# Keys of a gated delta rule turned by VectorE and a DMA through HBM instead of TensorE

## The chip, the cores and the metric

One core of a Trainium2 chip runs the whole kernel. The metric is the device time of one execution in microseconds (us), the median of several runs: 1523.45 us before the change (three runs, 1520.14 to 1526.65).

## What is computed

The input is x of 8 batches x 512 rows x 128 columns, all in f32. The output is

```
x = x + 0.5 * ffn(layernorm(x))        # gated: silu(x w1) * (x w2), two gelu layers of 512, back to 128
x = x + attn_block(layernorm(x))
x = x + 0.5 * ffn(layernorm(x))

attn_block(x):                         # 8 heads of 128
  n = layernorm(x)
  q, k = l2norm(silu(n Wq)), l2norm(silu(n Wk));  v = silu(n Wv)
  beta, alpha = sigmoid(n Wb), sigmoid(n Wa)
  per head and row t:  S = alpha (S - beta k (k S)) + beta k v;   o_t = S q_t
  x = x + o Wo
  x = x + gelu(layernorm(x) W1 + b1) W2 + b2
```

## The kernel before

**Chunks.** The recurrence is not run row by row. The 512 rows of a batch are cut into NC = 4 chunks of 128 rows (c = 0 to 3). For each chunk and each of the 8 heads the kernel forms the 128x128 products of keys with keys and of keys with queries, decays them, inverts the triangular matrix of the keys (on blocks of 32x32 on GpSimd, joined by TensorE), and then needs only a few 128x128 products per chunk to carry the state. A group g (0 or 1) is half of the heads, four, and fills one bank of PSUM.

**Stages.** Batches are worked in a software pipeline written out by hand, one queue of instructions for each engine. `SP(s, p, f1)` is the central stage: it runs the attention of batch s (solve, state, output: "S") and at the same time prepares batch p = s + 1 (projections, norms, keys: "P"); then come `F1(f1)` and `F2(s)`, the two feed-forward parts with the MLP, the products of keys with queries and the joins of the inverse among them. There are six such stages with p = 1 to 6 and f1 = p + 1, and one with p = 7 and no f1. Stage p = 1 follows a differently ordered first batch. SP has a first part (c = 0) and three steps (c = 1, 2, 3).

**TensorE in a step** (`SP_step`), each entry for both groups: products of keys with the state (L1386), projections of k (L1344), key products `keys_keys(p, c-1)` (L1364), `solve` (L1395), products of the state with the queries (L1412), `update` (L1403, not in c = 3), projections of q, `output` (L1422), projections of v, in c = 3 the turn of the next batch's input (L1231), `turn(p, c)` (L1356, 8 transposes of the keys against the identity), `attend` (L1431, the output projection). `SP_last` goes on with `keys_keys(p, 3)`, the four pairs of layer-1 products of f1 (L1267), the turn of the layer norm's rows xa (L1231), then the slots of F1. `layer1(…, 1)` waits for `attended` of c = 3 (its bank), `layer1(…, 2)` for the first gating.

**VectorE in a step**: `rhs` (L877), `squares` (L731 and three small ones: sums of squares of the keys of c and the queries of c - 1), `decayed_k(p, c-1)` (L843, key products times decays into R, R is also what `solve` reads), `new_state` (L885 and L889), `unit_k(p, c)` (L745: keys times 1/norm), `unit_q(p, c-1)` (L752, and then L757, a turn of 32x32 blocks of 128x1024 into the buffer mid), `attended` (L899). After step 3: moments of the layer norm (L590 to L603, L574 to L584), gating 0 (L641), rows xa (L609), gating 1, `decayed_k(p, 3)`, gating 2 and 3.

**GpSimd in a step**: `norm` (L482, a power), `scaled_k` (L501: keys times decays into KD, not in c = 3), `mask` (L491: growth rows plus the mask into MT; waits for the rows' DMA and for `output` of the same chunk). **ScalarE**: silu of k, `solved` (L1104), silu of q, output copies (L1109), silu of v, `copy_T` (L1098, turned keys from PSUM to KT), `decays` (L1082, eight exps on MT, waits for the mask).

**SP**, the queue of all DMAs, in order: for each c the blocks of R to HBM (L338), `q_store` (L355: mid to q_rows), growth rows (L330), `q_load` (L362: four loads that place the 32x32 blocks in QET so that the full turn is complete). The queries have gone this way already; the keys are turned on TensorE.

## Time and profile before

| what | value |
|---|---|
| profiled execution | 1525.31 us, of it 1523.6 us from the first to the last instruction |
| median of three runs | 1523.45 us |
| TensorE busy | 1447.8 us (95%); VectorE 810.8 (53%), ScalarE 692.2 (45%), GpSimd 566.2 (37%) |
| chain that ended last | TensorE 52%, issue 15%, GpSimd 13%, VectorE 12%, ScalarE 6% |
| granted TensorE clock | 0.974 of 2.4 GHz in the mean |
| stages p = 2 to 6 | the second half of layer 1 (L1267) starts at 441.20, 617.93, 794.67, 971.40 and 1148.12 us |
| DMA | 96.73 MB, 25.2% of the 16 engines' span |

Busy time is the union of an engine's instructions; that of TensorE includes time in which matmuls only drain. An f32 product of 128x128 is two matmul instructions in the trace, a transpose is one. An entry such as "[0.59 <-DVE big L641]" is the idle time of the engine ahead of the instruction and the instruction that ended it.

### The profile page before, as it was taken

To read this page: it belongs to the slowest core of one execution; us is meant where nothing else is said; L and a number is where in the kernel's file an instruction comes from. 1 tells how busy PE (TensorE), PEld (TensorE's weight loads), DVE (VectorE), ACT (ScalarE), POOL (GpSimd) and SP (SyncE) were. 2 spreads that over 40 slices of the span, in tenths; PEclk is the share of its full clock that TensorE was granted. 3 is DMA by queue.
4 is the path that set the end of the run, shared out by engine and by line. 5 is a ranking of instruction groups with operands and counts; after the bars stand their busy time and mean duration, and the time that the engine had idled before them with its cause. 6 is when DMAs were issued, how large, how long until landed. Compare 5 with 4: busy or idle time off the path is not lost.

```text
span 1523.6 us, 26080 instructions
## 1 busy us (share of the span) xinstructions
PE 1447.8 (95%) x10334; PEld 993.3 (65%) x10334; DVE 810.8 (53%) x2405; ACT 692.2 (45%) x1182; POOL 566.2 (37%) x641
## 2 busy tenths in 40 slices
PE   7997889999999999999999999999999999879968
PEld 3455776557866588566875578665885668645934
DVE  3566357553674556743674536654666436741330
ACT  2566256225662356424662266523664256622222
POOL 0037033741438124550338314471346504482000
PEclk9999699999999999999999999999999999889979
DMA  5122013230233214430232313331133302413000
GB/s 169 64 75 48 21 53 83 73 80 22 78 90 77 46 39 92 101 80 23 60 79 70 81 36 81 83 79 33 39 91 94 80 23 61 93 49 74 8 0 7
DMA packets 243338, 96.73 MB, mean 63 GB/s; under 512 B 212528, under 2 KB 227600, under 8 KB 243216
## 3 DMA queue, kind: packets, MB, share of 16 engines
q1 hardware_dynamic: 243216, 95.06, 25.2%
q8 instruction: 82, 1.34, 0.4%
q14 instruction: 40, 0.33, 0.1%
HBM read 65.43 MB, written 29.61 MB: 62 GB/s over the span
## 4 chain that ended last, share of the span: by engine, by line
PE 52%; issue 15%; POOL 13%; DVE 12%; ACT 6%; DMA 2%; SPq 0%; POOLq 0%; DVEq 0%; ACTq 0%
PE bank L1238 18%; PE bank L1344 4%; PE bank L1267 4%; POOL blkT L528 3%; POOL blkP L525 3%; PE bank L1246 3%; PE bank L1395 2%; DVE bst L731 2%; ACT MT L1082 2%; PE bank L1422 2%; POOL MT L491 2%; PE bank L1378 2%; PE bank L1431 2%; PE bank L1403 2%; PE bank L1614 1%
## 5 line engine op out<-in xcount | busy, mean ns | idle before, releaser
L1238 PE MATMUL bank<-big,h 128*128 128x512 f32 x992 | 447.0, 596 | 0.0
L1238 PEld LDWEIGHTS bank<-big,h 128*128 128x128 f32 x992 | 181.6, 190 | 197.0 <-issue 195.6
L482 POOL TENSOR_TENSOR rnorm<-ssq,mhalf 128x16 f32<-128x16 f32 (+1 forms) x35 | 84.0, 2401 | 539.4 <-DVE ssq L740 539.4
L1344 PE MATMUL bank<-wqkv,nT 128*128 128x512 f32 x336 | 161.5, 600 | 0.0
L528 POOL TENSOR_TENSOR blkT<-blkT,blkP 128x31 f32<-128x31 f32 (+15 forms) x248 | 135.9, 548 | 19.4
L525 POOL TENSOR_TENSOR blkP<-blkA,blkT 128x31 f32<-128x31 f32 (+15 forms) x248 | 126.4, 510 | 34.8 <-DMA blkA<-blocks_out 15.8
L1267 PE MATMUL bank<-xT,w 128*128 128x512 f32 x256 | 121.7, 622 | 7.6 <-ACT xT L996 4.2
L870 DVE TENSOR_SCALAR TB<-bank 32x512 f32<-32x512 f32 (+1 forms) x48 | 33.1, 689 | 144.6 <-PE bank L1656 64.8
L1013 ACT ACTIVATE big<-bank,cols 128x512 f32<-128x512 f32 x64 | 43.0, 686 | 138.3 <-PE bank L1238 100.4
L1020 ACT ACTIVATE big<-bank,cols 128x512 f32<-128x512 f32 x64 | 43.1, 686 | 108.6 <-PE bank L1238 108.5
L849 DVE TENSOR_TENSOR MT<-bank,MT 128x512 f32<-128x512 f32 x56 | 38.6, 691 | 99.6 <-PE bank L1378 99.6
L1267 PEld LDWEIGHTS bank<-xT,w 128*128 128x128 f32 x256 | 48.4, 200 | 65.2 <-issue 49.9
L1082 ACT ACTIVATE MT<-MT,biasj 128x128 f32<-128x128 f32 x256 | 78.3, 389 | 9.9 <-POOL MT L491 9.5
L509 POOL TENSOR_TENSOR QET<-QET,sgf 128x1024 f32<-128x1024 f32 x21 | 49.3, 2349 | 89.7 <-DMA sgf<-e_rows 89.7
L1344 PEld LDWEIGHTS bank<-wqkv,nT 128*128 128x128 f32 x336 | 57.0, 192 | 37.4 <-issue 36.8
L731 DVE BATCH_NORM_STATS2 bst<-big 128x6 f32<-128x128 f32 x224 | 46.0, 279 | 53.4 <-ACT big L1092 53.4
L1092 ACT ACTIVATE QET<-bank 128x512 f32<-128x512 f32 x56 | 33.5, 597 | 87.8 <-PE bank L1344 87.8
L491 POOL TENSOR_TENSOR MT<-rows_or_g,maskf 128x1024 f32<-128x1024 f32 x28 | 69.7, 2488 | 3.0 <-PE bank L1422 3.0
L1246 PE MATMUL bank<-w,big 128*128 128x128 f32 x512 | 68.2, 279 | 2.3 <-DVE TB L870 1.5
L1246 PEld LDWEIGHTS bank<-w,big 128*128 128x128 f32 x512 | 62.6, 192 | 11.8 <-issue 8.4
L1422 PEld LDWEIGHTS bank<-MT,V 128*128 128x128 f32 x512 | 61.8, 192 | 12.9 <-issue 12.9
L1395 PE MATMUL bank<-V,R 128*128 128x128 f32 x512 | 64.9, 281 | 2.8 <-DVE TB L870 1.6
(212 smaller groups left out, 2704.2 us busy)
## 6 DMA issues: line engine op xcount, KB each, us to landing
rows_or_g<-g_rows SPq DMA_DIRECT2D x28, 512.0 KB, 4.0
q_rows<-mid SPq DMA_DIRECT2D x28, 512.0 KB, 2.7
QET<-q_rows SPq DMA_DIRECT2D x112, 128.0 KB, 4.1
sgf<-e_rows SPq DMA_DIRECT2D x21, 512.0 KB, 4.7
blocks_out<-R SPq DMA_DIRECT2D x128, 32.0 KB, 1.7
blkA<-blocks_out SPq DMA_DIRECT2D x8, 512.0 KB, 3.2
t_back<-blkT SPq DMA_DIRECT2D x8, 512.0 KB, 2.6
r_back<-blkA SPq DMA_DIRECT2D x8, 512.0 KB, 3.0
```

The lines of the kernel that those rows point to most:

```text
L482: pool.tensor_tensor(rnorm[:, heads_of], ssq[:, heads_of], mhalf[:, :].to_broadcast([128, heads_of.stop - heads_of.start]), ALU.pow).then_ ...
L491: pool.tensor_tensor(MT[:, u, :], grow, maskf[:, :].unsqueeze(1).to_broadcast([128, H, 128]), ALU.add).then_inc(d_mask, 1)
L525: pool.tensor_tensor(prod, A3[:, j, j + 1:].unsqueeze(2).to_broadcast([128, n, m]), T3[:, j:j + 1, 0:m].to_broadcast([128, n, m]), ALU.mul ...
L528: pool.tensor_tensor(T3[:, j + 1:, 0:m], T3[:, j + 1:, 0:m], prod, ALU.subtract).then_inc(b_prod, 1)
L731: last = dve.bn_stats(bst[:, i, :], krow[g][:, i, :] if i < H else QET[:, H * (g - 1) + i - H, :])
L1082: last = act.activation(MT[:, u, :], MT[:, u, :], ACT.Exp, bias=biasj[:, u:u + 1])
L1238: last = pe.matmul(bank[bk + i][:, :], w[:, k, 128 * o:128 * o + 128], src[:, k, :], start=(k == 0), stop=(k == KB - 1))
L1246: last = pe.matmul(bank[4][:, 128 * c:128 * c + 128], src[:, k, 128 * c:128 * c + 128], w[:, k, :], start=(k == 0 and c == 0), stop=(k == ...
L1267: pe.matmul(bank[bk][:, :], w[:, 128 * o:128 * o + 128], xT[:, :], start=True, stop=True).then_inc(f["gate"], 1)
L1344: pe.matmul(bank[4 + n % 2][:, :], nT[:, 128 * c:128 * c + 128], wqkv[:, i // 2, 512 * (i % 2):512 * (i % 2) + 512], start=True, stop=True ...
L1395: last = pe.matmul(heads(bank[g])[:, h, :], R[:, u, :], V[:, u, :], start=True, stop=True)
L1422: last = pe.matmul(heads(bank[2 + g])[:, h, :], V[:, u, :], MT[:, u, :], start=(c == 0 and h == 0), stop=True, skip_group_check=True)
```

## The change

For the batches p = 1 to 7, all chunks but the last of the last batch (`at_end`), the keys no longer pass through TensorE and ScalarE. After `unit_k`, VectorE turns the 32x32 blocks of the keys into the chunk's part of R, which `solve` of batch s has read by then; SP stores it to a new tensor k_rows in HBM (`k_store`) and loads it back into KT by blocks (`k_load`, four DMAs). `keys_keys` waits for these loads. It is moved behind `update` in the steps c = 1 and 2, behind the projections of q in step 3, and, for chunk 3, from the head of `SP_last` to between the third and the fourth pair of layer-1 products. On VectorE `decayed_k` is moved behind `new_state`. The semaphores a_sq and a_sk become one counter each instead of four.

```diff
+def at_end(b, c):
+    return (b, c) == (B - 1, NC - 1)
...
+            def k_store(b, c):                                          # SP
+                sp.wait_ge(k_turned, (b - 1) * NC + c + 1)
+                sp.dma_start(k_rows[c, :, :], R[:, H * c:H * c + H, :].rearrange("p h n -> p (h n)")).then_inc(k_out, 16)
+            def k_load(b, c):
+                sp.wait_ge(k_out, 16 * ((b - 1) * NC + c + 1))
+                if c > 0:
+                    sp.wait_ge(s_ks, (b - 1) * 6 + 2 * c)
+                blocked = k_rows[c, :, :].rearrange("(r x) (u k p) -> k x u r p", r=NBLK, u=H, k=NBLK)
+                for k in range(NBLK):
+                    sp.dma_start(KT[BS * k:BS * k + BS, H * c:H * c + H, :].rearrange("x u (r p) -> x u r p", r=NBLK),
+                                 blocked[k]).then_inc(k_in[c % 2], 16)
...
             def P(b):
-                grow_in(b, 1)
+                k_store(b, 0), k_load(b, 0), grow_in(b, 1)
                 for c in range(1, NC):
                     blocks(b, c - 1)
+                    if not at_end(b, c):
+                        k_store(b, c)
                     q_store(b, c - 1)
+                    if not at_end(b, c):
+                        k_load(b, c)
...
             def unit_k(b, c):                                           # VectorE
...
+                if at_end(b, c):
+                    return
+                dve.wait_ge(p_unit, b * NC + c + 1)
+                dve.wait_ge(s_w, (b - 1) * 8 + 2 * c + 2)
+                dve.transpose(R[:, H * c:H * c + H, :].rearrange("p h n -> p (h n)"), krow[c].rearrange("p h n -> p (h n)")
+                              ).then_inc(k_turned, 1)
...
             def SP_step(s, p, c):                                       # VectorE
                 rhs(s, c, 0), rhs(s, c, 1)
                 if p is not None:
-                    squares(p, c), decayed_k(p, c - 1)
+                    squares(p, c)
                 if c < NC - 1:
                     new_state(s, c, 0), new_state(s, c, 1)
                 if p is not None:
+                    decayed_k(p, c - 1)
                     unit_k(p, c), unit_q(p, c - 1)
                 attended(s, c)
...
-                    copy_T(p, c, 0), copy_T(p, c, 1), decays(p, c)      # ScalarE, SP_step; SP_first alike
+                    if at_end(p, c):
+                        copy_T(p, c, 0), copy_T(p, c, 1)
+                    decays(p, c)
...
             def keys_keys(b, c, g):                                     # TensorE
-                pe.wait_ge(p_trc, 2 * NC * (b + 1) + 2 * c + g + 1)
+                if at_end(b, c):
+                    pe.wait_ge(p_trc, 4 * NC + g + 1)
+                elif g == 0:
+                    pe.wait_ge(k_in[c % 2], 16 * NBLK * (2 * (b - 1) + c // 2 + 1))
+                if c > 0:
+                    pe.wait_ge(p_dk, b * 2 * NC + 2 * c - 1 + g)
+                else:
+                    pe.wait_ge((j_dve, j_act)[g], b * NS)
...
             def SP_step(s, p, c, f1):
                 state_keys(s, c, 0), state_keys(s, c, 1)
                 if p is not None:
-                    proj(p, c, 2), proj(p, c, 3), keys_keys(p, c - 1, 0), keys_keys(p, c - 1, 1)
+                    proj(p, c, 2), proj(p, c, 3)
...
                 if c < NC - 1:
                     update(s, c, 0), update(s, c, 1)
+                elif p is not None:
+                    proj(p, c, 0), proj(p, c, 1)
                 if p is not None:
+                    keys_keys(p, c - 1, 0), keys_keys(p, c - 1, 1)
+                if c < NC - 1 and p is not None:
                     proj(p, c, 0), proj(p, c, 1)
                 output(s, c, 0), output(s, c, 1)
...
-                    turn(p, c, 0), turn(p, c, 1)
+                    if at_end(p, c):
+                        turn(p, c, 0), turn(p, c, 1)
                 attend(s, c)
...
             def SP_last(s, p, f1):
-                if p is not None:
+                if f1 is None and p is not None:
                     keys_keys(p, NC - 1, 0), keys_keys(p, NC - 1, 1)
                 if f1 is not None:
                     layer1("f1", f1, 0)
                     pe.wait_ge(s_xa, s * NC + NC)
-                    layer1("f1", f1, 1), layer1("f1", f1, 2), layer1("f1", f1, 3)
+                    layer1("f1", f1, 1), layer1("f1", f1, 2), keys_keys(p, NC - 1, 0), keys_keys(p, NC - 1, 1)
+                    layer1("f1", f1, 3)
```

## Rows read from the trace of the kernel before

**Rows 1.** The page, part 1: busy us (share of the span) and instructions.
```profile
PE 1447.8 (95%) x10334; PEld 993.3 (65%) x10334; DVE 810.8 (53%) x2405; ACT 692.2 (45%) x1182; POOL 566.2 (37%) x641
```

**Rows 2.** TensorE's groups by line: count, busy us, mean ns, idle before.
```profile
L1356 PE MATMUL bank<-ident,big 128*128 128x128 f32 x224 | 30.0, 278 | 7.1 <-DVE R L870 3.8 <-DVE big L745 3.4
```

**Rows 3.** Timeline of TensorE, stage p = 3: start us, us, line.
```profile
574.45 1.95 PE L1431 MATMUL bank<-wo,blkA 128*128 128x128 f32 x16
...
592.98 1.95 PE L1431 MATMUL bank<-wo,blkA 128*128 128x128 f32 x16
...
609.29 1.04 PE L1356 MATMUL bank<-ident,big 128*128 128x128 f32 x8
610.16 1.95 PE L1431 MATMUL bank<-wo,blkA 128*128 128x128 f32 x16
611.95 1.95 PE L1364 MATMUL bank<-KT 128*128 128x128 f32 x16
613.74 3.60 PE L1267 MATMUL bank<-xT,w 128*128 128x512 f32 x8
617.93 3.70 PE L1267 MATMUL bank<-xT,w 128*128 128x512 f32 x8 [0.59 <-DVE big L641]
621.47 0.60 PE L1231 MATMUL bank<-ident,xa 128*128 128x128 f32 x4
```

**Rows 4.** The chain of waits, 545 to 640 us, in order of time.
```profile
581.71 3.20 DVE bst L731 x16
...
588.76 1.23 DVE big L745
...
592.83 2.36 POOL MT L491
...
600.10 3.20 DVE bst L731 x16
...
604.04 2.92 POOL rnorm L482
...
608.12 3.39 DVE QET L752
611.54 1.25 DVE mid L757
...
617.12 0.76 DVE big L641
```

**Rows 5.** Timelines of VectorE and GpSimd, end of stage p = 1.
```profile
252.55 3.36 DVE L745 TENSOR_TENSOR big<-big,rnorm 128x1024 f32<-128x1024 f32 x1 [1.82 <-POOL rnorm L482]
...
252.48 2.34 POOL L491 TENSOR_TENSOR MT<-rows_or_g,maskf 128x1024 f32<-128x1024 f32 x1
```

**Rows 6.** Timelines of VectorE and GpSimd, 626 to 629 us.
```profile
626.36 2.29 DVE L752 TENSOR_TENSOR QET<-QET,rnorm 128x1024 f32<-128x1024 f32 x1 [1.76 <-POOL rnorm L482]
...
627.52 1.22 POOL L525 TENSOR_TENSOR blkP<-blkA,blkT 128x31 f32<-128x31 f32 x1
```

**Rows 7.** Timelines of TensorE and GpSimd, stage p = 1.
```profile
195.03 1.94 PE L1356 MATMUL bank<-ident,big 128*128 128x128 f32 x8 [3.77 <-DVE R L870]
...
255.96 1.09 PE L1356 MATMUL bank<-ident,big 128*128 128x128 f32 x8 [2.81 <-DVE big L745]
...
199.71 1.90 POOL L501 TENSOR_TENSOR KD<-big,kds 128x1024 f32<-128x1024 f32 x1 [10.42 <-issue]
```

**Rows 8.** Windows of 2 us: busy us of each engine, then granted clock, DMA.
```profile
192.00:194.00 2.00, 0.00 (x0) 0.00 (x0) 1.96 (x5) 0.00 (x0) 0.00 (x0) 0.84 0.00 0
...
198.00:200.00 2.00, 2.00 (x12) 2.00 (x11) 0.00 (x0) 1.57 (x5) 0.29 (x1) 0.50 0.01 4
...
254.00:256.00 2.00, 0.04 (x1) 0.04 (x1) 2.00 (x2) 0.00 (x0) 0.82 (x1) 1.00 0.00 0
```

**Rows 9.** DMA: SP's timeline, and the page's issues with us to landing.
```profile
615.84 2.80 SPq L362 DMA_DIRECT2D QET<-q_rows  x4
...
QET<-q_rows SPq DMA_DIRECT2D x112, 128.0 KB, 4.1
```

More of the change, by code:

```diff
@@ L193, in build_program @@
         g_rows = nc.dram_tensor("g_rows", [U, C], f32).ap()
+        k_rows = nc.dram_tensor("k_rows", [NC, 128, H * 128], f32).ap()
         q_rows = nc.dram_tensor("q_rows", [NC, 128, H * 128], f32).ap()
@@ L238, in build_program @@
         a_unit, a_qnorm, a_knorm = sem("a_unit"), sem("a_qnorm"), sem("a_knorm")
-        a_sq, a_sk = ([sem(f"a_{k}{i}") for i in range(4)] for k in ("sq", "sk"))
+        a_sq, a_sk = sem("a_sq"), sem("a_sk")
         a_gate, a_rows = ([sem(f"a_{k}{c}") for c in range(NC)] for k in ("gate", "rows"))
@@ L247, in build_program @@
         q_in = [sem("q_in0"), sem("q_in1")]
+        k_turned, k_out = sem("k_turned"), sem("k_out")
+        k_in = [sem("k_in0"), sem("k_in1")]
         n_eT, e_out, e_in, s_sq = sem("n_eT"), sem("e_out"), sem("e_in"), sem("s_sq")
@@ L765, in moments0 @@
                 if c == NC - 1:
-                    last.then_inc((a_sq, a_sk)[x][0], 1)
+                    last.then_inc((a_sq, a_sk)[x], 1)
             def norms0(x):
                 done = (a_sq, a_sk)[x]
-                dve.wait_ge(done[0], 1)
-                dve.tensor_tensor(bsq0, bst0[:, :, 1::3], bst0[:, :, 1::3], ALU.mult).then_inc(done[1], 1)
-                dve.wait_ge(done[1], 1)
+                dve.wait_ge(done, 1)
+                dve.tensor_tensor(bsq0, bst0[:, :, 1::3], bst0[:, :, 1::3], ALU.mult).then_inc(done, 1)
+                dve.wait_ge(done, 2)
                 dve.scalar_tensor_tensor(out=bsq0, in0=bsq0, scalar=64.0, in1=bst0[:, :, 2::3],
-                                         op0=ALU.mult, op1=ALU.add).then_inc(done[2], 1)
-                dve.wait_ge(done[2], 1)
+                                         op0=ALU.mult, op1=ALU.add).then_inc(done, 1)
+                dve.wait_ge(done, 3)
                 ssq_x, rnorm_x = (z[:, x, :, :].rearrange("p c h -> p (c h)") for z in (ssq0, rnorm0))
                 dve.scalar_tensor_tensor(out=ssq_x, in0=bsq0[:, :, 0], scalar=EPS_L2, in1=bsq0[:, :, 1],
-                                         op0=ALU.add, op1=ALU.add).then_inc(done[3], 1)
-                dve.wait_ge(done[3], 1)
+                                         op0=ALU.add, op1=ALU.add).then_inc(done, 1)
+                dve.wait_ge(done, 4)
                 rsqrt((a_qnorm, a_knorm)[x], 0, ssq_x, rnorm_x, rs_ta[:, :], rs_tb[:, :])
@@ L1096, in copy_T @@
                 u = slice(H * c + 4 * g, H * c + 4 * g + 4)
-                act.wait_ge(p_tr, 2 * NC * (b + 1) + 2 * c + g + 1)
+                act.wait_ge(p_tr, 4 * NC + g + 1)
                 act.activation(KT[:, u, :], heads(bank[6 + g]), ACT.Copy).then_inc(p_trc, 1)
@@ L1178, in SP_first @@
                 if p is not None:
-                    silu(p, 0, 4), silu(p, 0, 5), copy_T(p, 0, 0), copy_T(p, 0, 1)
+                    silu(p, 0, 4), silu(p, 0, 5)
                     if p == 1:
@@ L1350, in turn, with keys_keys @@
                     pe.wait_ge(p_unit, b * NC + c + 1)
+                pe.wait_ge(p_dk, b * 2 * NC + 2 * c - 1 + g)
+                for h in range(4):
+                    last = pe.transpose(bank[6 + g][:, 128 * h:128 * h + 128], krow[c][:, 4 * g + h, :], ident[:, :])
+                last.then_inc(p_tr, 1)
+            def keys_keys(b, c, g):
+                if at_end(b, c):
+                    pe.wait_ge(p_trc, 4 * NC + g + 1)
+                elif g == 0:
+                    pe.wait_ge(k_in[c % 2], 16 * NBLK * (2 * (b - 1) + c // 2 + 1))
                 if c > 0:
@@ L1354, in turn @@
                     pe.wait_ge((j_dve, j_act)[g], b * NS)
-                for h in range(4):
-                    last = pe.transpose(bank[6 + g][:, 128 * h:128 * h + 128], krow[c][:, 4 * g + h, :], ident[:, :])
-                last.then_inc(p_tr, 1)
-            def keys_keys(b, c, g):
-                pe.wait_ge(p_trc, 2 * NC * (b + 1) + 2 * c + g + 1)
                 for h in range(4):
@@ L1456, in SP_first @@
                 if p is not None:
-                    proj(p, 0, 4), proj(p, 0, 5), turn(p, 0, 0), turn(p, 0, 1)
+                    proj(p, 0, 4), proj(p, 0, 5)
                 attend(s, 0)
```

## The prediction
> **What bounds the kernel now.** I read the page first: TensorE is busy for 95% of the span [rows 1], and the turns of the keys are one of its groups [rows 2]. That suggests that whatever TensorE is spared comes off the time. The view that decides is the chain of waits over one of the repeating stages (prepare batch p beside attention of batch s = p - 1). I take p = 3, from 545 to 640 us; stages p = 2 to 6 repeat every 176.7 us to within 0.1 us.
>
> In the steps c = 1 and 2 TensorE is full: from one output projection (L1431) to the next it takes 592.98 - 574.45 = 18.53 us [rows 3]. But the chain does not run through it. It is a loop over three engines: squares of the keys on VectorE (L731), norms on GpSimd (L482), `unit_k` (L745), scaled keys on GpSimd (L501), mask (L491), exps and the next silus on ScalarE, squares again. From squares to squares it takes 600.10 - 581.71 = 18.39 us [rows 4], only 0.14 less than TensorE's step, with hardly a wait in it. After the last step (c = 3) the chain stays on VectorE: norms end at 606.96, then `unit_k`, `unit_q` (held until the mask is done, 3.39 us instead of 1.22), the block turn of the queries (1.25), `attended`, the moments of the layer norm and the first gating, which starts at 617.12 [rows 4]. Only then can TensorE run the second pair of layer-1 products: it idled 0.6 us before them, from 617.34 to 617.93 [rows 3]. So the end of a stage is set by VectorE's chain, and TensorE is covered up to there by work that it has to do anyway.
>
> **The change part by part.**
>
> *Turns removed from TensorE.* 27 of 28 chunks lose 8 transposes: 610.16 - 609.29 = 0.87 us each time [rows 3], 23.5 us in all, and the waits ahead of them, 7.1 us in sum, all of it in stage p = 1 [rows 2]. In stages 2 to 6 that is 4 x 0.87 = 3.5 us before TensorE reaches the first layer-1 products; it comes there too early, because the first gating doesn't move forward. ScalarE's copies of KT go too; they lie in the time in which it waits for the mask, and I cost them at nothing.
>
> *Block turn added to VectorE.* `unit_k` is followed by a 128x1024 block turn, and `unit_q`, the queries' own turn and `attended` stand behind it in the queue. The same operation took 1.25 us in each case [rows 4]. It works beside GpSimd undisturbed, so scaled keys can start as before. In steps 1 and 2 VectorE has room: `attended` comes some 2 us later, at about TensorE's next products with the state, and `rhs` still ends before `solve` needs it by a few tenths. In step 3 there is no room. Norms end at 607.0 as before (I add 0.1 for the drift of two rounds). `output` is now done before that, so GpSimd's mask no longer waits for it, but takes the memory first, and `unit_k` is held. That is the order of stage p = 1, where the mask began at 252.48 and `unit_k`, begun at 252.55, took 3.36 us [rows 5]. So: norms 607.1, mask and `unit_k` +3.4 = 610.5, block turn +1.2 = 611.7, `unit_q` +1.2 = 612.9, its turn +1.2 = 614.1, against 612.7 before. Mask, `unit_k` and `unit_q` cost the same in either order; the difference is the added turn: +1.4 us with the drift.
>
> *The wait moved in front of layer 1.* From there the moments and the gating take as long as before: gating starts at 614.1 + 4.4 = 618.5, and its product pair on TensorE at 619.3 instead of 617.93. Before it, TensorE is done with the output projection between 608.5 (all 3.5 us saved) and 609.4 (a wait of 0.8 us before `update` in step 2, where ScalarE's silus end late for the earlier TensorE). It does one layer-1 pair (1.72), waits for `attended` until 614.4, does the second pair, waits again for the gating until 619.3: two gaps of about 3.3 and 3.2 us, where there was one of 0.6.
>
> *Key products moved.* The products of chunk 3 took 613.74 - 611.95 = 1.79 us ahead of layer 1 [rows 3]; there they filled the time in which the gating was made. Now they stand between the third and the fourth layer-1 pair, behind the gating. The stretch behind it grows from 3.45 to 3.45 + 1.79 us. So TensorE leaves the stage at 619.3 + 5.24 = 624.55 instead of 621.4: +3.15 us. In steps 1 to 3 the products move by a few places within one full queue; they are worth nothing there. Behind the stage TensorE is full and the inversion and its transfers have room, so 3.15 us stay.
>
> *Transfers.* A chunk adds a store of 512 KB and four loads of 128 KB on SP's queue. k_load stands behind q_store, which waits for the queries' turn. In steps 1 and 2 the loads can go out some 0.5 us after that turn; they take 2.8 us to issue [rows 9] and 4.1 us to land [rows 9], about 1 to 2 us before the moved products want them. For chunk 3 the loads start at 614.6, the last at 616.7, and land at 620.8; they are wanted at 621.0. I take nothing; the bounds are 0 and 2 us per stage. The growth rows, now behind k_load, have 8 us of room.
>
> *Stages p = 1 and 7.* In p = 1 the scaled keys started at 199.71, because an exp stood behind the copies of KT, and these behind the turn at 195.03 [rows 7]. Without it they can start when `unit_k` ends, at 194.3: the loop starts 5.4 us earlier. At the stage's end 0.2 of it goes to VectorE's longer chain and 1.8 to the moved products: -3.4 us (bounds: 0 and -7.1, all the waits before turns). In p = 7 the last turn stays on TensorE and waits for a held `unit_k`: +0.7 us (bounds 0 and 3).
>
> *Clock.* With an idle time of 3.77 us before the turn at 195.03 the granted clock fell from 2.4 to 1.2 GHz within the wait (0.84 in one window, 0.50 in the next ones) and stayed there until about 200.1: 5.1 us of work at half rate, 2.5 us lost [rows 7, 8]. With 2.81 us before the turn at 255.96 it did not fall [rows 7, 8]. The new gaps of 3.3 and 3.2 us with 1.7 us of work between them lie between these two. The cost is 0 to 2.5 us per stage for six stages; I take the middle, 1.25 each, 7.5 us. The Trainium skill (TensorE: Matmul & The Clock Gate, Part 1) says "the default state is throttled, and activity releases the throttle", and advises against idle gaps between bursts of matmuls; by that rule all six stages pay in full, +15 us in place of 7.5.
>
> *Sum*, against the profiled execution's own 1525.31 us (span 1523.6): -3.4 + 5 x 3.15 + 0.7 = +13.0, clock +7.5, together +20.5: 1545.8. The median of the runs is 1.9 us below that execution, so the forecast is 1544 us.
>
> **The rivals.**
>
> *A, faster: TensorE is the bound and what it is spared counts.* Then 23.5 + 7.1 = 30.6 us go: 1493 us. For it: 95% busy and a chain with 52% on TensorE. Against it: the chain of the stage's end is VectorE's, and the products that follow the gating have become more. It decides if the first gating comes at least 1.8 us earlier than now; nothing on its chain gets shorter. 10%.
>
> *B, no change: the memory goes to GpSimd twice in a row.* In steps 1 and 2 `unit_q` now waits while the scaled keys run, and the mask is queued right behind them. At 626.36 in the same situation VectorE got its turn in between: GpSimd's next operation of 31 elements, begun at 627.52, took 1.22 us [rows 6]. If the mask went first instead, the loop would win about 0.9 us a round, norms of step 3 would end some 1.7 us earlier, and a stage would cost 1.4 us instead of 3.15: -3.4 + 7 + 0.7 = +4.3, 1528 us without a fallen clock. 10%.
>
> *C, slower still: the keys come late.* SP issues in order and the two stores and eight loads of a step meet in the DMA engines. If the loads of chunk 3 land 2 us late in six stages, the time is 1544 + 12 = 1556 us. For it: a margin of 0.2 us there. Against it: loads of the same pattern from q_rows took 4.1 us in the median over 112 [rows 9]. 18%. The Trainium skill (VectorE: DVE Perf Modes, The three transpose paths) warns that a plain DMA copy that turns by its access pattern is 19 times slower than the crossbar's turn. By it every product of keys would wait for tens of us and the kernel would be far slower than here; the loads from q_rows, whose shortest runs are the same, show no such thing, and I give it less than 1% inside C.
>
> **How the numbers follow.** Forecast 62%, with its own range of 1536.5 (the clock never falls) to 1551.5 (it falls in all six); A 10%, B 10%, C 18%. A measurement of this kernel tells about 0.5% (7.6 us) from no change. A is the case faster; B lies within it; the forecast and C are slower: 0.10, 0.10, 0.80. The range from 1526 to 1560 leaves out A and the upper end of C.
>
> **What would show it.** Right: per stage two idle times of TensorE on the L1267 products, one released by VectorE's `attended` (L899) or its successor, one by the gating (L641), together 5 to 7 us where 0.6 stood; `unit_k` of step 3 held to about 3.4 us; the period of stages 2 to 6 grown from 176.7 to between 179.9 and 182.4 us; squares to squares still 18.4 us; a granted clock below 1.0 in slices that now show 9s. Wrong: L641 releasing TensorE no later than now relative to the stage's start; a period under 176.7; waits of the key products on the loads of KT in steps 1 and 2 above 1 us; or `rhs` late enough to hold `solve` by more than 1 us, which would raise the price of the added turn beyond mine.

## The result, and the profile after

The changed kernel is slower: 1549.45 us (median of 4 runs, 1548.85 to 1554.82) beside 1524.22 us for the kernel before (median of 4), ratio 1.0176 with a 95% interval of 1.0144 to 1.0208. The forecast was 1544 us, with a range of 1526 to 1560. From the first to the last instruction, the profiled execution of after takes 1547.1 us; before took 1523.6, so 23.5 us are to be explained.

The page of after, part 1, answers to [rows 1]. The 27 turns are gone from TensorE (216 instructions, 23.5 us), but its busy time fell by only 5.3 us:

```profile
PE 1442.5 (93%) x10118; PEld 976.4 (63%) x10118; DVE 850.7 (55%) x2432; ACT 662.1 (43%) x1128; POOL 565.8 (37%) x641
```

TensorE's groups by line (count, busy us, mean ns, then the idle time before them by releaser). L1303 are the layer-1 products (L1267 of before), L1404 the key products (L1364):

```profile
L1303 PE MATMUL bank<-xT,w 128*128 128x512 f32 x256 | 137.8, 681 | 34.8 <-DVE xa L932 18.7 <-DVE big L668 11.9 <-ACT xT L1030 4.2
...
L1404 PE MATMUL bank<-KT 128*128 128x128 f32 x448 | 58.0, 285 | 0.3 <-DMA KT<-k_rows 0.3
```

The 7.1 us of idle time ahead of the turns [rows 2] are gone, and ahead of layer 1 TensorE waits 30.6 us for VectorE, 18.7 released by `attended` (L932) and 11.9 by the gating (L668). Before had 7.6 us of idle time there in all, 4.2 of it the same wait for ScalarE. For the keys through HBM, TensorE waited 0.3 us in the whole program.

TensorE's timeline at the end of stage p = 3 (start us, us; in brackets the idle time ahead and its releaser), which answers to [rows 3]:

```profile
610.16 0.60 PE L1267 MATMUL bank<-ident,xin 128*128 128x128 f32 x4
610.60 1.95 PE L1471 MATMUL bank<-wo,blkA 128*128 128x128 f32 x16
612.39 1.88 PE L1303 MATMUL bank<-xT,w 128*128 128x512 f32 x4
617.41 1.98 PE L1303 MATMUL bank<-xT,w 128*128 128x512 f32 x4 [3.14 <-DVE xa L932]
622.32 3.18 PE L1303 MATMUL bank<-xT,w 128*128 128x512 f32 x4 [2.93 <-DVE big L668]
625.29 2.48 PE L1404 MATMUL bank<-KT 128*128 128x128 f32 x16
627.61 1.88 PE L1303 MATMUL bank<-xT,w 128*128 128x512 f32 x4
629.33 0.60 PE L1267 MATMUL bank<-ident,xa 128*128 128x128 f32 x4
```

Two gaps of about 3 us, the products between them, and a third pair that takes 3.18 us where the second took 1.98. VectorE over the same time, answering to the end of [rows 4]:

```profile
610.14 3.38 DVE L772 TENSOR_TENSOR big<-big,rnorm 128x1024 f32<-128x1024 f32 x1 [1.82 <-POOL rnorm L509]
613.55 1.25 DVE L778 STREAM_TRANSPOSE R<-big 128x1024 f32<-128x1024 f32 x1
614.72 1.18 DVE L785 TENSOR_TENSOR QET<-QET,rnorm 128x1024 f32<-128x1024 f32 x1
615.94 1.25 DVE L790 STREAM_TRANSPOSE mid<-QET 128x1024 f32<-128x1024 f32 x1
617.11 0.25 DVE L932 TENSOR_TENSOR xa<-bank,xa 128x128 f32<-128x128 f32 x1
...
621.52 0.75 DVE L668 SCALAR_TENSOR_TENSOR big<-bank,cols,sgf 128x512 f32<-128x512 f32 x1
```

and GpSimd, in step 1 and at the end of the stage:

```profile
574.68 1.90 POOL L528 TENSOR_TENSOR KD<-big,kds 128x1024 f32<-128x1024 f32 x1 [1.49 <-DVE big L772]
576.54 3.35 POOL L518 TENSOR_TENSOR MT<-rows_or_g,maskf 128x1024 f32<-128x1024 f32 x1
...
607.20 2.91 POOL L509 TENSOR_TENSOR rnorm<-ssq,mhalf 128x16 f32<-128x16 f32 x1 [8.86 <-DVE ssq L767]
610.07 2.36 POOL L518 TENSOR_TENSOR MT<-rows_or_g,maskf 128x1024 f32<-128x1024 f32 x1
```

The mask starts 0.07 us ahead of `unit_k`, which takes 3.38 us instead of 1.22; the turn, `unit_q` and the second turn follow one behind the other. In windows of 2 us the granted clock (the first number behind the engines' busy times) falls right behind the second gap, from 2.4 to 1.2 GHz, that is from 1.0 to 0.5:

```profile
621.00:623.00 2.00, 0.68 (x2) 0.44 (x3) 1.90 (x8) 0.00 (x0) 0.00 (x0) 0.99 0.96 150
623.00:625.00 2.00, 2.00 (x4) 0.75 (x3) 0.95 (x3) 0.69 (x1) 0.00 (x0) 0.50 1.13 153
625.00:627.00 2.00, 2.00 (x12) 1.71 (x11) 0.02 (x1) 0.00 (x0) 0.00 (x0) 0.65 0.95 112
```

It is like this in stages p = 3 and 4. In the four others the clock fell in or right behind the first gap, of 2.6 us (p = 1) or 3.2 us (p = 2, 5, 6), before the second had begun. In p = 2, 5 and 6 it was still low for the third pair. TensorE in p = 2, where the granted clock is 0.50 from 436 to 444 us:

```profile
434.58 3.17 PE L1303 MATMUL bank<-xT,w 128*128 128x512 f32 x4 [3.25 <-DVE xa L932]
439.50 3.78 PE L1303 MATMUL bank<-xT,w 128*128 128x512 f32 x4 [1.75 <-DVE big L668]
```

A landmark makes the kernels comparable: the turns of `xin` on TensorE (610.16 here) split a stage into its full part and its end, which closes with the turns of `xa` (629.33). The table has stage p = 3 of every kernel and the mean of the four periods from p = 2 to p = 6, both from the one profiled execution, and the medians of all executions:

| kernel | xa to xin | xin to xa | mean period | median us (before beside it) | ratio, 95% interval |
|---|---|---|---|---|---|
| before | 164.11 | 12.62 | 176.73 | | |
| after | 162.43 | 19.17 | 182.00 | 1549.45 (1524.22) | 1.0176, 1.0144 to 1.0208 |
| e1 | 161.49 | 15.20 | 177.53 | 1521.31 (1523.25) | 0.998, 0.9967 to 0.9994 |
| e2 | 164.11 | 12.83 | 176.95 | 1528.39 (1523.25) | 1.0033, 1.002 to 1.0045 |
| e3 | 164.11 | 14.42 | 179.37 | 1539.57 (1523.25) | 1.0117, 1.0085 to 1.0148 |
| e4 | 162.34 | 17.86 | 180.17 | 1537.93 (1523.25) | 1.0102, 1.0076 to 1.0128 |
| e5 | 162.32 | 18.33 | 180.30 | 1536.37 (1522.62) | 1.0094, 1.0064 to 1.0124 |
| e6 | 162.32 | 16.33 | 179.91 | 1538.30 (1522.62) | 1.0097, 1.0078 to 1.0116 |
| e7 | 162.96 | 15.20 | 178.11 | 1529.72 (1522.62) | 1.0039, 1.0021 to 1.0058 |
| e8 | 163.67 | 12.91 | 176.40 | 1517.14 (1522.62) | 0.9951, 0.9933 to 0.9969 |
| e9 | 164.27 | 12.48 | 177.68 | 1530.24 (1523.89) | 1.0042, 1.0026 to 1.0058 |
| e10 | 163.43 | 12.91 | 176.10 | 1516.55 (1523.89) | 0.9945, 0.9928 to 0.9963 |
| e11 | 162.98 | 13.04 | 175.99 | 1513.50 (1523.89) | 0.9923, 0.9908 to 0.9938 |
| e12 | 164.11 | 12.48 | 176.60 | 1520.06 (1522.83) | 0.998, 0.9966 to 0.9994 |

After is 1.68 us shorter in the full part and 6.55 us longer at the end. The experiments ask what makes the end.

One caution for reading two traces against each other. The first batch, up to the first projections of stage p = 1 (L1344 at 189.27 us in before, L1380 at 188.79 in after), does the same work in all kernels. Yet in the profiled executions it ends anywhere from 185.3 us (e4) to 194.0 (e3), and the granted clock fell in it at different times. So the differences of stages below are counted from that point on.

### The profile page after: what moved, and what is told of

Read it like the earlier page. It is cut to its first block, busy times and chain, and to the rows that moved or that the text cites. A ratio compares the mean times of both kernels' runs of the same rounds, so it can differ in the third digit from the quotient of the medians.

```text
span 1547.1 us, 25805 instructions
## 1 busy us (share of the span) xinstructions
PE 1442.5 (93%) x10118; PEld 976.4 (63%) x10118; DVE 850.7 (55%) x2432; ACT 662.1 (43%) x1128; POOL 565.8 (37%) x641
## 3 DMA queue, kind: packets, MB, share of 16 engines
q1 hardware_dynamic: 359424, 123.38, 34.3%
q8 instruction: 80, 1.31, 0.3%
## 4 chain that ended last, share of the span: by engine, by line
issue 37%; POOL 29%; PE 19%; DVE 10%; ACT 4%; DMA 2%; POOLq 0%; DVEq 0%; ACTq 0%
POOL blkT L555 7%; PE bank L1274 7%; POOL blkP L552 6%; POOL rnorm L509 5%; POOL MT L518 4%; POOL QET L536 3%; POOL KD L528 2%; DVE bst L758 2%; PE bank L1303 2%; DVE big L772 2%; ACT MT L1116 1%; DMA sgf<-e_rows 1%; PE bank L1282 1%; PE bank L1571 1%; POOL blkA L558 1%
## 5 line engine op out<-in xcount | busy, mean ns | idle before, releaser
L1303 PE MATMUL bank<-xT,w 128*128 128x512 f32 x256 | 137.8, 681 | 34.8 <-DVE xa L932 18.7
L1380 PE MATMUL bank<-wqkv,nT 128*128 128x512 f32 x336 | 161.5, 600 | 0.0
L1303 PEld LDWEIGHTS bank<-xT,w 128*128 128x128 f32 x256 | 50.8, 213 | 98.3 <-issue 50.7
L1380 PEld LDWEIGHTS bank<-wqkv,nT 128*128 128x128 f32 x336 | 57.0, 192 | 37.4 <-issue 35.4
L518 POOL TENSOR_TENSOR MT<-rows_or_g,maskf 128x1024 f32<-128x1024 f32 x28 | 79.8, 2850 | 0.0
L1435 PEld LDWEIGHTS bank<-V,R 128*128 128x128 f32 x512 | 63.2, 196 | 15.0 <-issue 12.5
L1282 PEld LDWEIGHTS bank<-w,big 128*128 128x128 f32 x512 | 62.6, 192 | 11.8 <-issue 8.4
```

The source lines that it names most:

```text
L518: pool.tensor_tensor(MT[:, u, :], grow, maskf[:, :].unsqueeze(1).to_broadcast([128, H, 128]), ALU.add).then_inc(d_mask, 1)
L1282: last = pe.matmul(bank[4][:, 128 * c:128 * c + 128], src[:, k, 128 * c:128 * c + 128], w[:, k, :], start=(k == 0 and c == 0), stop=(k == ...
L1303: pe.matmul(bank[bk][:, :], w[:, 128 * o:128 * o + 128], xT[:, :], start=True, stop=True).then_inc(f["gate"], 1)
L1380: pe.matmul(bank[4 + n % 2][:, :], nT[:, 128 * c:128 * c + 128], wqkv[:, i // 2, 512 * (i % 2):512 * (i % 2) + 512], start=True, stop=True ...
L1435: last = pe.matmul(heads(bank[g])[:, h, :], R[:, u, :], V[:, u, :], start=True, stop=True)
```

## The experiments

**e1: before without the turns.** TensorE's turns and ScalarE's copies are left out from batch 1 on, so the key products use old keys.

```diff
-                    turn(p, c, 0), turn(p, c, 1)
-                    ... copy_T(p, c, 0), copy_T(p, c, 1), decays(p, c)
+                    ... decays(p, c)
```

> The kernel before without any turn of the keys of batches 1 to 7 on TensorE and without ScalarE's copies of them (left out: KT keeps the first batch's keys, so the products of the later batches use those). Nothing is put on VectorE or the DMAs. If the end of a stage is set by VectorE's chain, the 3.5 us that TensorE is spared in each of the stages 2 to 6 buy nothing there (second layer-1 pair still 176.7 us apart) and only stage 1 wins, about 5 us: 1518 us. If TensorE is the bound (rival A), 23.5 + 7.1 us go: 1493 us.

Measured 1521.31, ratio 0.998. Freeing TensorE of all turns is worth 2 us, not 30: the first theory is held, rival A falls. The 2 us are a difference of two effects. In the profiled executions stage p = 1 got 6.3 us shorter, and p = 2 to 6 got 4.9 us longer together, because the clock fell in p = 2, 4 and 6 (1.7 us each). TensorE in stage p = 3, where it held:

```profile
604.76 2.05 PE L1369 MATMUL bank<-KT 128*128 128x128 f32 x16 [1.78 <-DVE big L745]
...
612.25 3.70 PE L1267 MATMUL bank<-xT,w 128*128 128x512 f32 x8 [2.01 <-DVE big L641]
```

The full part became 2.62 us shorter (three turns of 0.87), the end 2.58 us longer: what TensorE is spared ahead of VectorE's chain it spends in waiting for that chain.

**e2: before with the block turn added.** TensorE still turns the keys; VectorE turns them as well, behind `unit_k`.

```diff
                 dve.tensor_tensor(krow[c], krow[c], rnorm... ).then_inc(p_unit, 1)
+                dve.wait_ge(p_unit, b * NC + c + 1)
+                dve.wait_ge(s_w, (b - 1) * 8 + 2 * c + 2)
+                dve.transpose(R[...], krow[c]...).then_inc(k_turned, 1)
```

> The kernel before, turns on TensorE kept, with the added block turn of 128x1024 behind unit_k on VectorE (written into R, read by nothing). VectorE's chain at a stage's end is 1.25 us longer, and the first gating and the stage end 1.3 us later in each of five stages, 0.5 to 1.3 in the other two: 1523.5 + 8 = 1531 us. If VectorE's added work is hidden, 1524 us.

Measured 1528.39. It lies between the two, but the trace decides against the theory's reason: a steady stage grew by 0.22 us, not by 1.25. Of the rest, 3.1 us lie in stage p = 1: an idle time of 5.03 us ahead of the first turn replaced the 3.77 of [rows 7], and the clock fell behind a wait of 2.98 us, where before it held behind 2.81. VectorE and GpSimd at the end of p = 3:

```profile
612.19 1.22 DVE L746 TENSOR_TENSOR big<-big,rnorm 128x1024 f32<-128x1024 f32 x1 [1.79 <-POOL rnorm L483]
613.45 1.25 DVE L750 STREAM_TRANSPOSE R<-big 128x1024 f32<-128x1024 f32 x1
614.62 2.11 DVE L757 TENSOR_TENSOR QET<-QET,rnorm 128x1024 f32<-128x1024 f32 x1
```

```profile
612.44 3.20 POOL L492 TENSOR_TENSOR MT<-rows_or_g,maskf 128x1024 f32<-128x1024 f32 x1 [0.29 <-PE bank L1428]
```

Here the mask still waits for `output` and comes behind `unit_k`. It runs while VectorE turns, and `unit_q`, which the mask would have held for 2.2 us in any case [rows 4], is held for only 0.9 us. From the end of the norms to the start of `attended` it is 5.78 us, against 5.77 in before and 7.00 in after.

**e3: before with the key products of chunk 3 moved** between the third and the fourth layer-1 pair.

```diff
-                    keys_keys(p, NC - 1, 0), keys_keys(p, NC - 1, 1)
                 if f1 is not None:
-                    ... layer1("f1", f1, 2), layer1("f1", f1, 3)
+                    ... layer1("f1", f1, 2), keys_keys(p, NC - 1, 0), keys_keys(p, NC - 1, 1)
+                    layer1("f1", f1, 3)
```

> The kernel before with one edit: the key products of chunk 3 stand between the third and fourth layer-1 pair instead of at the head of SP_last. TensorE waits for the first gating 0.6 + 1.8 = 2.4 us instead of 0.6, and the stage ends 1.8 us later, six times: 1523.5 + 10.7 = 1534 us. If the products only change places within a full queue, 1524 us.

Measured 1539.57, 5 to 6 us more than the theory's. TensorE:

```profile
630.73 1.98 PE L1267 MATMUL bank<-xT,w 128*128 128x512 f32 x4 [2.40 <-DVE big L641]
632.55 1.95 PE L1364 MATMUL bank<-KT 128*128 128x128 f32 x16
```

The products left a gap of 2.40 us where 0.59 stood and cost their 1.8 us behind it. The remainder is the clock, as far as the trace shows: in three of the five stages p = 2 to 6 the stretch from the third pair to the turns of `xa` took 7.0 us, in the other two 5.32. The trace is of the slowest of four executions (1547.85 us), and 4.8 us of its excess lie in the first batch.

**e4: after with both gaps filled** by three products of 128x512 each, whose results nobody reads.

```diff
                     layer1("f1", f1, 0)
+                    pe.wait_ge(p_dk, p * 2 * NC + 2 * NC - 2)
+                    filler(3)
                     pe.wait_ge(s_xa, s * NC + NC)
-                    layer1("f1", f1, 1), layer1("f1", f1, 2), keys_keys...
+                    layer1("f1", f1, 1), filler(3), layer1("f1", f1, 2), keys_keys...
```

> The changed kernel with three products of 128x512 of constant data (weights w1 and w2 into a bank that is free) in each of the two gaps of TensorE ahead of attended and of the first gating: 2.6 us of work in gaps of 3.2 and 2.9 us. If the gaps themselves cost nothing beyond VectorE's chain but let the clock fall, the clock stays at 2.4 GHz there and what half rate cost comes back: the five stages 2 to 6 repeat every 179.9 us instead of 181.6 to 182.9, about 10 to 13 us in all, 1538 us. If the clock costs nothing, 1549 us; if the filler delays TensorE, more.

Measured 1537.93, 11.5 us under after with more work. Between the profiled executions it is 13.5 us, 3.5 of them in the first batch, so some 10 us are what the clock cost. From 240 to 1330 us the granted clock is 1.00, and the pairs behind the gaps take 1.98 us in each stage:

```profile
610.75 1.98 PE L1303 MATMUL bank<-xT,w 128*128 128x512 f32 x4 [0.64 <-DVE xa L932]
...
615.66 1.98 PE L1303 MATMUL bank<-xT,w 128*128 128x512 f32 x4 [0.35 <-DVE big L668]
```

**e5: after, the mask of chunk 3 behind `unit_k`.**

```diff
                 pool.wait_ge(s_o, s * 8 + 2 * c + 2)
+                if c == NC - 1:
+                    pool.wait_ge(p_unit, b * NC + c + 1)
                 pool.tensor_tensor(MT[:, u, :], grow, maskf... )
```

> After, with one wait more: GpSimd's mask of chunk 3 also waits for unit_k(3), so that VectorE scales the keys first, turns them while GpSimd works, and only then scales the queries. In the trace of after GpSimd's mask (610.07) stood ahead of unit_k (610.14, 3.38 us), and turn, unit_q and turn followed one behind the other; in the run with a turn added to the kernel before, where unit_k came ahead of the mask, the added turn cost 0.2 us a stage. Theory: the turn costs its 1.25 us only because of that order. Then unit_k(3) takes 1.18, the turn lies under the mask, and the attended rows come about 1.2 us earlier in each of six stages: 1549.5 - 7 = 1542 us, with attended at about 1.0 us after the end of the queries' turn as now. Rival: the turn costs 1.25 us in whatever order (VectorE's own time is the bound), or the mask's later end holds ScalarE's exponentials and with them the silu of layer 1: no change, 1549, or slower, 1553.

Measured 1536.37: one wait more gives 13 us. VectorE, end of p = 3:

```profile
605.83 1.23 DVE L774 TENSOR_TENSOR big<-big,rnorm 128x1024 f32<-128x1024 f32 x1 [1.82 <-POOL rnorm L509]
607.09 1.25 DVE L780 STREAM_TRANSPOSE R<-big 128x1024 f32<-128x1024 f32 x1
608.26 2.41 DVE L787 TENSOR_TENSOR QET<-QET,rnorm 128x1024 f32<-128x1024 f32 x1
```

The turn lies under the mask (607.23, 2.36 us), as in e2; norms to `attended` went from 7.00 to 6.08 us and the first gap from 3.14 to 2.31. The mechanism is the theory's and the gain is nearly twice its 7 us. In the profiled executions each of the stages p = 2 to 6 gave 1.8 us (0.9 of it on the chain, 0.9 at TensorE's clock, by the measure of the next section), and p = 7 gave 2.1: there, too, the mask had held a `unit_k` for which TensorE waited. Stage p = 1 gave nothing: its first gap got 1.1 us shorter, and the fallen clock took as much again.

**e6: after without chunk 3's block turn** on VectorE (the unturned keys are stored).

```diff
-                if at_end(b, c):
+                if c == NC - 1:
                     return
```

> After, with the block turn of chunk 3's keys left out on VectorE (the DMA stores the unturned keys, so chunk 3's key products are of rows in another order; batches 1 to 6). Theory: a VectorE turn of 1.25 us in the path to attended(3) costs its length: 1549.5 - 6 x 1.25 = 1542 us; the rest of the loss (key products 1.79 us a stage and the slower TensorE clock) stays. Rival: the turn is not on the path, and the loss is all of the moved key products and the clock: 1549.

Measured 1538.30. Norms to `attended` fell from 7.00 to 5.73 us: with the mask first, the turn costs its whole length. The other 4 us below the theory are about what the clock gave back: it took 6.6 us in p = 2 to 6 instead of after's 11.3. Turn and order cost 1.25 us only when they meet: norms to `attended` is 5.77 us with neither (before), 5.78 with the turn alone (e2), 5.73 with the mask first alone (e6) and 7.00 with both.

**e7: chunk 3 back on TensorE**, with its products ahead of layer 1; chunks 0 to 2 by the new route.

```diff
 def at_end(b, c):
-    return (b, c) == (B - 1, NC - 1)
+    return b > 0 and c == NC - 1
...
-                    ... layer1("f1", f1, 2), keys_keys(p, NC - 1, 0), keys_keys(p, NC - 1, 1)
+                    ... layer1("f1", f1, 2), layer1("f1", f1, 3)
```

> After, but chunk 3's keys are turned by TensorE and copied by ScalarE as in the kernel before, and its key products stand again ahead of layer 1; chunks 0 to 2 keep VectorE's turn, the route through HBM and the later key products. Theory: the whole loss arises at chunk 3, where VectorE's order sets the end of the stage; chunks 0 to 2 lie under TensorE's waits, as the run without any turns showed (1521 us). Then the loss goes and stage p = 1 keeps its 3 us: 1521 us (1518 to 1525). Rival: VectorE's turns and the transfers cost in every chunk alike, and three quarters of the loss stay: 1542 us.

Measured 1529.72 (1523.82 to 1534.06). 20 of the 25 us are gone, so the loss does arise at chunk 3; but 1521 was expected. TensorE waited in a new place, in six of the seven stages:

```profile
610.19 1.09 PE L1389 MATMUL bank<-ident,big 128*128 128x128 f32 x8 [2.27 <-DVE big L772]
```

The three turns that TensorE is spared bring `output` forward, and the mask (606.71) again stands ahead of `unit_k` (606.77, 3.37 us).

**e8: e7 with three orders changed.** VectorE does `attended(3)` and the layer norm ahead of `unit_q(2)`; TensorE turns chunk 3 behind the first layer-1 pair and multiplies it behind the second.

```diff
-                    unit_k(p, c), unit_q(p, c - 1)
+                    unit_k(p, c)
+                    if c < NC - 1 or f1 is None:
+                        unit_q(p, c - 1)
...
-                gating("f1", f1, 0), LN_M_rows(s), gating("f1", f1, 1), decayed_k(p, NC - 1)
+                gating("f1", f1, 0), LN_M_rows(s), gating("f1", f1, 1), unit_q(p, NC - 2), decayed_k(p, NC - 1)
...
+                    layer1("f1", f1, 0), turn(p, NC - 1, 0), turn(p, NC - 1, 1)
                     pe.wait_ge(s_xa, s * NC + NC)
+                    layer1("f1", f1, 1), keys_keys(p, NC - 1, 0), keys_keys(p, NC - 1, 1)
```

> As the run with chunk 3 back on TensorE, and besides: on VectorE the queries of chunk 2 are scaled and turned behind the gating of layer 1's second block, so that attended(3) and the moments come right behind unit_k(3); on TensorE chunk 3's turn stands behind attend(3) and layer 1's first block, and its key products behind the second block; ScalarE copies the turned keys behind the first silu of layer 1. Theory: the stage ends when attended(3) and its moments allow, and unit_q and its turn (1.2 to 3.4 us and 1.25 us) leave that path, while TensorE's work fills the wait: 2 us less in each of six stages, and a clock that holds: 1507 us (1503 to 1512). Rival: what was taken off the path comes back behind it, in the gating of blocks 2 and 3 and in the first slots of the next FFN: 1520 us, as with chunk 3 back alone.

Measured 1517.14: faster than both kernels, but 10 us short of the theory and nearer to the rival's 1520. The end fell to 12.91 us with `attended` no longer late, and the clock held in p = 2 to 6. Now other releasers hold TensorE, the keys' loads in p = 2, 3 and 4 and the copies of chunk 3 in each stage:

```profile
593.39 2.05 PE L1406 MATMUL bank<-KT 128*128 128x128 f32 x16 [1.07 <-DMA KT<-k_rows]
...
606.37 2.05 PE L1406 MATMUL bank<-KT 128*128 128x128 f32 x16 [0.89 <-ACT KT L1134]
```

**e9: before with e8's order on VectorE alone** (the first two edits of e8).

> The kernel before with VectorE's order alone changed in the stages that carry layer 1 (p = 1 to 6): unit_q(2) and its turn stand behind the gating of layer 1's second block instead of ahead of attended(3), as in the 1517 us version, while TensorE turns all keys and the key products stand where they stood. Theory: in the kernel before, attended(3) came at 612.71 against attend's end at 612.1, and the only wait of TensorE that this path sets is the 0.59 us ahead of layer 1's third block; so the reorder alone gives at most 0.6 us a stage: 1520 us (1518 to 1523). Rival: the gain of the 1517 us version is this reorder, and the new route of the keys gives nothing: 1517 or less.

Measured 1530.24: slower, which neither expected. The end of the stage did get 0.14 us shorter (12.48). But the queries of chunk 2 are now stored 10.6 us later (612.81 against 623.43), and SyncE does all else behind them: the reload of the blocks for GpSimd's inversion is issued at 632.97 instead of 623.82, and GpSimd's last scaling of queries starts at 694.50 instead of 685.56. There it meets a layer norm of VectorE. VectorE, then GpSimd, then TensorE:

```profile
694.66 0.87 DVE L590 BATCH_NORM_STATS2 lnf_st<-xin 128x6 f32<-128x128 f32 x4
695.57 1.31 DVE L594 TENSOR_TENSOR lnf_mean<-lnf_st 128x4 f32<-128x4 f32 x1
```

```profile
694.50 2.35 POOL L509 TENSOR_TENSOR QET<-QET,sgf 128x1024 f32<-128x1024 f32 x1 [4.40 <-DMA sgf<-e_rows]
```

```profile
701.66 1.13 PE L1240 MATMUL bank<-big,h 128*128 128x512 f32 x2 [0.64 <-DVE R L870]
```

An operation of 128x4 elements took 1.31 us instead of 0.17, and a join behind it held TensorE, in four stages by 0.64 to 1.53 us, 4.1 us in sum. That chain is read from the trace; no run took it away by itself. Another 2.9 us of the profiled execution lie in stage p = 1, where the clock fell behind a wait of 2.82 us; before had 2.81 there and it held [rows 7]. Whether that belongs to the edit is open.

**e10: e8 with the keys' load ahead of the queries' store** on SyncE.

```diff
                         k_store(b, c)
+                        k_load(b, c)
                     q_store(b, c - 1)
-                    if not at_end(b, c):
-                        k_load(b, c)
```

> The 1517 us version with SyncE's order changed: the load of a chunk's turned keys stands ahead of the queries' store of the chunk before. In its trace the keys' load of chunk 2 was issued at 585.24, behind the queries' store at 584.80, and TensorE waited 1.07 us for it at 593.39 (0.68 us in the stage before). Theory: the load starts about 1 us earlier and the wait goes: 1517 - 6 x 0.9 = 1512 us (1509 to 1515). Rival: SyncE then stands at the landing of the keys' store instead, the queries' store, the growth rows and the queries' loads come 3 us later, and the mask or the key-query products wait: 1517 or more.

Measured 1516.55, no difference from e8 that can be told. The theory's 1512 was missed. The waits for the keys' DMA in p = 2, 3 and 4 are gone and the period fell by 0.3 us, not by 0.9; TensorE's waits for VectorE's joins in the FFN rose from 1.2 us in one place to 2.6 in three.

**e11: e7 with e5's wait.**

> The version with chunk 3 back on TensorE (1529.7 us), with GpSimd's mask of chunk 3 waiting for unit_k(3) as well. In its trace unit_k(3) took 3.37 us beside the mask (606.71, 2.35 us), and TensorE waited 2.27 us at the turn of chunk 3, where the kernel before waited for nothing and unit_k took 1.22 us. Theory: the 7 us over the kernel before are this order of the two engines; unit_k falls to 1.2 us, the wait to about 0.2 us, and the stage to 176 us: 1529.7 - 6 x 2 = 1518 us (1515 to 1521). Rival: the 7 us come from the chunks' transfers and later key products (waits of 0.36 and 0.54 us a stage) and from the later mask: 1528 to 1530.

Measured 1513.50, the fastest kernel of the study and 1.5 us below the theory's range; here the two engines' order is worth 16 us. VectorE and GpSimd:

```profile
598.43 1.23 DVE L774 TENSOR_TENSOR big<-big,rnorm 128x1024 f32<-128x1024 f32 x1 [1.82 <-POOL rnorm L509]
599.57 1.22 DVE L787 TENSOR_TENSOR QET<-QET,rnorm 128x1024 f32<-128x1024 f32 x1
```

```profile
599.83 3.20 POOL L520 TENSOR_TENSOR MT<-rows_or_g,maskf 128x1024 f32<-128x1024 f32 x1 [1.43 <-DVE big L774]
```

Neither of VectorE's multiplications is held any more: the mask comes 0.26 us behind the start of `unit_q` and waits itself. TensorE's waits for `unit_k` at the turns fell from 14.5 us in six places to 2.4 in four, and the clock, which in e7 had fallen in p = 2, 6 and 7 behind such waits, held in p = 1 to 6.

**e12: before with e5's wait alone.**

> The kernel before with one wait more: GpSimd's mask of chunk 3 also waits for unit_k(3). In its trace the mask was called at 607.45, while unit_k (606.98, 1.22 us) ran, and had the memory ahead of unit_q, which took 3.38 us; with the wait the mask is called at 608.4, when unit_q (608.12) has the memory, so that unit_q takes 1.2 us, the queries' turn ends 2.1 us earlier and the mask about 0.8 us later. Theory: TensorE waits in these stages for 0.59 us ahead of layer 1's third block and for nothing else, so the order gives at most that here, and the 10 us of the version at 1513.5 us come from the keys' new route together with the order: 1520 us (1518 to 1523). Rival: the order of mask and VectorE alone gives those 10 us: 1514.

Measured 1520.06, as forecast. The wait by itself gives 2.8 us, though hardly where the theory has it: a steady stage got only 0.14 us shorter, p = 7 1.0 us and p = 1 1.9, its wait for `unit_k` ahead of the turn of chunk 3 being 0.68 us instead of 2.81. The new route of chunks 0 to 2 on top of the wait gives 6.6 more (e11; 7.6 when each median is set against that of the kernel before beside it). In the profiled executions 5.2 us of the route's gain lie in stage p = 1 and 3.1 in the next five together, while e11's first batch was 2.0 us longer. "The route" is here all that e11 and e12 differ in: turns, transfers, and the later key products and `decayed_k`; no run takes them apart.

## Why the prediction was right, and where it was not

*What bounds the stage's end.* Right. Squares to squares took 18.46 us (18.39 before), TensorE was spared 23.5 us and the kernel got slower, and e1 shows that sparing it alone is worth 2. Counted from the start of stage p = 3, 2.99 us later in after, `attended`, gating and third pair come at 614.12, 618.53 and 619.33 us; forecast were 614.1, 618.5 and 619.3.

*The terms.* The part at full clock can be told from the rest: from the second layer-1 pair to the turns of `xa` it is 10.24 us where the clock held (e6, 611.25 to 621.49), and in after's six stages 10.76, 13.15, 11.92, 11.90, 13.22 and 12.28. The excess, 11.8 us, is put down to the clock; e4, which held it, got some 10 back. Then:

| term | forecast | measured |
|---|---|---|
| first batch | 0 | -0.5 |
| stage p = 1 | -3.4 | -3.1 |
| p = 2 to 6, each | +3.15 | +3.17 |
| p = 7 | +0.7 | +0.8 |
| behind p = 7 | 0 | -1.3 |
| clock | +7.5 | +11.8 |
| sum | +20.5 | +23.5 |

The -1.3 us behind p = 7 were not traced to a cause; over the profiled executions of all kernels that part takes 195.4 to 198.3 us. The forecast took 3.45 us for the stretch from the third pair to `xa`, where [rows 3] give 3.54; as it used the same figure on both sides, nothing changes.

The step "I take the middle, 1.25 each" of the clock is the one that was mis-sized: it fell in every one of the six stages, at 2.0 us each in the mean. The bounds of 0 and 2.5 us came from a gap that did and a gap that did not drop the clock, read as if the length of the gap decided. The lower bound rested on one execution: behind the wait of 2.81 us at which it held in before [rows 7] it fell in e3 and, at 2.82, in e9:

```profile
260.75 1.97 PE L1356 MATMUL bank<-ident,big 128*128 128x128 f32 x8 [2.81 <-DVE big L745]
```

And in four of after's six stages the first gap alone was enough. A pair that is slow ahead of the gating costs nothing by itself, since the second gap gets shorter by as much (1.75 us in p = 2 instead of 2.93); what counts is what is still slow behind it. The Trainium skill (TensorE: Matmul & The Clock Gate, Part 1), weighed in the prediction, says that activity is what keeps the clock up. On whether it falls the trace of after agrees, six times of six, though with gaps of 2.3 and 2.9 us it held in one stage of e5; on the price the forecast's "all six stages pay in full, +15 us" is 3 us too high, since a stage lost 0.5 to 3.0 us.

*The added turn.* The size was right: `attended` stands 1.23 us later behind the norms, and the gating 1.4 us later in the stage, as forecast. The reason was half right. "Mask, `unit_k` and `unit_q` cost the same in either order; the difference is the added turn" holds without a turn between them (5.77 us in before, 5.73 in e6). With one, the order decides: a turn that follows `unit_k` and precedes the held `unit_q` is free (e2), and the same turn behind a held `unit_k` costs its length (after, e6). The price belongs to the meeting of two edits, and one wait on GpSimd takes most of it back (e5). The same order, brought on by an earlier `output`, is what kept e7 from its 1521. Of the two operations that meet, the one that started first took its own time and the other waited: `unit_k`, begun 0.07 us behind the mask, took 3.38 us, and the mask, begun 0.26 us behind `unit_q` (e11), took 3.20, where each alone takes 1.2 and 2.36. The Trainium skill (SBUF — State Buffer, SBUF: two separate sides) calls the memory port pair that VectorE and GpSimd share "an **exclusive lock**, not a bandwidth split", and gives it to whichever starts first; these traces agree.

*The moved products.* Right: e3 shows 1.8 us a stage and the gap they left.

*Rivals.* A is refuted by e1. B is refuted by after's step 1: between GpSimd's two operations (574.68 and 576.54) VectorE's `unit_q` got the memory, and the mask took 3.35 us for it:

```profile
575.80 1.85 DVE L785 TENSOR_TENSOR QET<-QET,rnorm 128x1024 f32<-128x1024 f32 x1
```

C is refuted for after by the 0.3 us on L1404; in the faster kernels, where TensorE comes to the key products earlier, the loads do hold it, by up to 1.15 us (e8). What none of them held is that the same route can win: with chunk 3 kept on TensorE and the mask behind `unit_k`, the new route for 21 of 28 chunks takes part in a gain of 10 us (6.6 of them, e11 against e12), more than half of it in stage p = 1, which is not one of the repeating stages.

Left open: why a gap of the same length drops the clock in one stage and not in the next (2.0 us in e1, 2.4 in e3, 2.8 in p = 1), and e9's long way round.

## What to carry to other kernels

Work taken from a busy engine was worth nothing ahead of a wait that another engine sets (e1); work moved from ahead of such a wait to behind it cost its full length and opened a gap (e3). Before adding an operation between two that contend with another engine, ask which side comes first after the change: an engine that becomes free earlier may start its next operation in front of the one that matters, and a wait added to the less urgent one can then be worth more than the work that was saved (by the medians 13 us in e5, 16 in e11, from one wait). Where a chain's last round differs from the others, treat it apart: here three of four chunks gained by the new route, once the mask was held back, and the fourth lost more.

## What the runs showed of the hardware beyond the forecast

- A block turn of 128x1024 in f32 on VectorE took 1.25 us in every trace and neither held GpSimd nor was held by it: the mask of e5 (607.23, 2.36 us) and the scaled keys of after (574.68, 1.90 us) ran beside it.
- The clock's fall is not decided by a gap's length alone. With 2.4 us ahead of the third pair it fell in three of five stages (e3), with 2.0 us in every other one (e1); with 2.0 and 2.9 us and one pair between them it held in one stage of e6 and fell in the four others with these gaps. Behind 2.8 us in p = 1 it held in before and fell in e3 and e9. Where it fell behind the last gap it cost up to 1.7 us of a stretch of 5.3; where it fell at the first and lasted over the third pair, 2.0 to 3.0 us (after, p = 2, 5, 6).
- In after the added transfers cost no more than 0.3 us of waits of TensorE: the stores of 512 KB landed in 2.6 us and the loads of 128 KB with their axes turned in 4.0 us (medians over 27 and 108), while the queue's share of the DMA engines rose from 25.2% to 34.3%. The transfers beside them got slower: the growth rows landed in 4.8 us instead of 4.0, the queries' loads in 4.3 instead of 4.1.
